# Seven PSUM banks of an attention and expert kernel: by the slot at which a reader is due, instead of in turn, with new slot tables

## The reference

```python
x = x + mlstm(layernorm(x), ctx, ctx)            # 4 heads of 64, gates, decays, a norm
x1 = layernorm(x)
n1 = ln(x1)                                      # one block of attention and experts
probs = softmax(mean(n1) @ rw + rb)              # over M = 2 attentions of 16 heads of 16
att = softmax(q k^T / 4) v, for each m and head; out = sum_m probs[m] * (att wo[m] + bo[m])
y = x1 + out
n2 = ln(y); p, i = top_k(softmax(mean(n2) @ ffn_rw + ffn_rb), 2)
x = x + y + sum_k p[k] * gelu(n2 @ fw1[i[k]]) @ fw2[i[k]]
```

## Time and profile before

| | |
|---|---|
| median of three runs | 1423.33 us (1421.33 to 1429.55) |
| profiled execution | span 1426.9 us, granted clock 0.990; the page has no other time of it |
| to the first score | 85.7 us |
| first period | 145.2 us |
| middle periods | 166.8, 167.1, 169.7, 167.1, 167.3, 167.2 us |
| last period's 128 scores | 133.1 us |
| after them | 57.7 us |
| busy share PE, DVE, ACT, POOL | 98%, 77%, 64%, 25% |

### The profile page before, as it was taken

How to read it: one execution, slowest core, us unless ns; L and a number is a source line. 1 busy time by engine, 2 the same in 40 slices (tenths; PEclk the granted TensorE clock), 3 DMA queues, 4 the chain that set the end, 5 groups by cost and what they waited for, 6 DMA issues and landing times.

```text
span 1426.9 us, 22218 instructions
## 1 busy us (share of the span) xinstructions
PE 1393.6 (98%) x7666; PEld 716.9 (50%) x7666; DVE 1092.2 (77%) x2299; ACT 916.4 (64%) x1706; POOL 363.6 (25%) x351
## 2 busy tenths in 40 slices
PE   8999899999999999999999999999999999999999
PEld 5643434455454654555445554455545454454456
DVE  5779977987789877987779877797769986786721
ACT  3266557766677666675677765876666766757752
POOL 6512342203313123132241133130331322330000
PEclk9999999999999999999999999999999999999999
DMA  4056037430854127441464308541084413561002
GB/s 116 17 70 95 2 45 107 71 62 16 104 76 76 45 38 112 75 75 31 51 101 69 64 31 101 79 75 46 24 102 70 78 56 45 73 77 46 17 1 89
DMA packets 92308, 90.15 MB, mean 63 GB/s; under 512 B 16483, under 2 KB 87267, under 8 KB 91295
## 3 DMA queue, kind: packets, MB, share of 16 engines
q1 hardware_dynamic: 92196, 88.73, 38.6%
HBM read 35.05 MB, written 4.25 MB: 28 GB/s over the span
## 4 chain that ended last, share of the span: by engine, by line
PE 69%; issue 8%; DVE 4%; DMA 3%; SPq 2%; POOL 1%; ACT 1%; DVEq 0%; POOLq 0%; ACTq 0%
PE psum L881 12%; PE psum L866 12%; PE psum L851 12%; PE psum L819 7%; PE psum L838 6%; PE psum L701 5%; PE psum L452 5%; PE psum L736 3%; DMA qst<-mrow 3%; PE psum L475 2%; SPq L1954 2%; PE psum L563 2%; DVE mx L1378 1%; PE psum L573 1%; DVE x L1293 1%
## 5 line engine op out<-in xcount | busy, mean ns | idle before, releaser
L1378 DVE TENSOR_REDUCE mx<-psum 128x1 f32<-128x512 f32 x1024 | 645.5, 681 | 134.2 <-PE psum L851 133.5
L1677 ACT ACTIVATE prob<-psum 128x512 f32<-128x512 f32 x1024 | 568.2, 600 | 270.8 <-PE psum L881 159.4
L866 PE MATMUL psum<-qst,kst 98*128 98x512 bf16 x1024 | 355.9, 383 | 10.5 <-DMA qst<-mrow 8.7
L851 PE MATMUL psum<-kst,qst 96*128 96x512 bf16 x1024 | 318.8, 381 | 2.9 <-DVE resid L1252 1.3
L881 PE MATMUL psum<-prob,vst 128*17 128x512 f32 x2048 | 248.1, 601 | 2.7 <-ACT prob L1677 2.3
L866 PEld LDWEIGHTS psum<-qst,kst 98*128 98x128 bf16 x1024 | 96.9, 99 | 220.8 <-issue 126.9
L851 PEld LDWEIGHTS psum<-kst,qst 96*128 96x128 bf16 x1024 | 99.0, 98 | 121.2 <-issue 17.9
L881 PEld LDWEIGHTS psum<-prob,vst 128*17 128x17 f32 x2048 | 46.7, 97 | 136.3 <-issue 106.8
L838 PE MATMUL psum<-w,cxT 128*128 128x256 f32 x448 | 105.4, 381 | 0.0
L819 PE MATMUL psum<-n2T,x 128*128 128x512 f32 x224 | 103.0, 592 | 0.0
L1828 POOL CAST parts<-resid 128x512 bf16<-128x512 f32 x64 | 41.0, 640 | 239.9 <-DVE resid L1252 239.9
(11 more groups left out here) (244 smaller groups left out, 1761.5 us busy)
## 6 DMA issues: line engine op xcount, KB each, us to landing
kst<-parts SPq DMA_DIRECT2D x186, 128.0 KB, 4.7
qst<-parts SPq DMA_DIRECT2D x186, 128.0 KB, 5.9
cmat<-G_dram SPq DMA_DIRECT2D x7, 1024.0 KB, 4.6
x<-in_L_ffn_fw SPq DMA_DIRECT2D x14, 512.0 KB, 3.7
w<-in_L_ffn_fw SPq DMA_DIRECT2D x14, 512.0 KB, 4.2
xbuf<-in_x SPq DMA_DIRECT2D x8, 512.0 KB, 5.1
kin<-in_ctx SPq DMA_DIRECT2D x8, 512.0 KB, 4.5
out<-acc SPq DMA_DIRECT2D x7, 512.0 KB, 9.0
```

The source lines that it names most:

```text
L851: e.matmul(psum[:, u.bank, :], qst[0:KROWS, h, t * P:(t + 1) * P], kst[0:KROWS, h, :], start=True, stop=True).then_inc(u.full, 1)
L866: e.matmul(psum[:, u.bank, :], kst[0:KROWS + 2, h, g * P:(g + 1) * P], qst[0:KROWS + 2, h, :], start=True, stop=True).then_inc(u.full, 1)
L1378: e.tensor_reduce(mx[:, qq * QUAD + j, t:t + 1], psum[:, u.bank, :], AX, ALU.max).then_inc(u.free, 1)
L1677: e.activation(prob[:, g % 2, j, :], psum[:, u.bank, :], ACT.Exp).then_inc(u.free, 1)
```

## The change

Each use now gets the bank whose last use has the earliest due slot (until), the longest unused one among equals; TensorE waits for that bank's last use. The due slot of a side piece's use is the slot of its reader in the tables (freed_at), at least the slot after the take; that of any other use is the slot after the take, and before the first slot all are equal. The values' bank is bank 7 instead of 6. All tables are new, for PE, ACT, DVE, POOL and SP, and so is AHEAD. VectorE's max_index waits for the expert loads of the batch before. What is computed is the same. Cut to what the prediction speaks of (the tables of POOL, SP and the second half, and ACT's others, are new in the same way):

```diff
 class Use:
-    def __init__(self, bank, n, full, free):
-        self.bank, self.n, self.full, self.free = bank, n, full, free
-class Ring:
-    def __init__(self, banks, full, free):
-        self.banks, self.full, self.free, self.n, self.uses = banks, full, free, 0, {}
-    def take(self, *name):
-        k, n = self.n % len(self.banks), self.n // len(self.banks)
-        self.n += 1
+    def __init__(self, bank, n, full, free, was, until):
+        self.bank, self.n, self.full, self.free, self.was, self.until = bank, n, full, free, was, until
+class Banks:
+    def __init__(self, count, full, free):
+        self.count, self.full, self.free, self.uses = count, full, free, {}
+        self.counts, self.latest, self.order, self.taken = [0] * count, [None] * count, [-1] * count, 0
+    def until(self, k):
+        return self.latest[k].until if self.latest[k] is not None else -1000
+    def take(self, name, until):
         assert name not in self.uses
-        self.uses[name] = Use(self.banks[k], n + 1, self.full[k], self.free[k])
-        return self.uses[name]
+        k = min(range(self.count), key=lambda k: (self.until(k), self.order[k]))
+        self.counts[k] += 1
+        self.taken += 1
+        self.order[k] = self.taken
+        use = Use(k, self.counts[k], self.full[k], self.free[k], self.latest[k], until)
+        self.uses[name] = self.latest[k] = use
+        return use
...
-        RB, VB = (0, 1, 2, 3, 4, 5, 7), 6
-        bank_full = [sem(f"bank_full_{k}") for k in range(len(RB))]
-        bank_free = [sem(f"bank_free_{k}") for k in range(len(RB))]
-        ring = Ring(RB, bank_full, bank_free)
-        uses = ring.uses
+        VB = 7
+        bank_full = [sem(f"bank_full_{k}") for k in range(VB)]
+        bank_free = [sem(f"bank_free_{k}") for k in range(VB)]
+        banks = Banks(VB, bank_full, bank_free)
+        uses = banks.uses
...
         FIRST = dict(
-            PE_A=slots(-8, "kT0:4 kT1:0 qT0:0 qT1:0 gates:7 gsum:18 cols:26 cd0:0 cd1:3 st0:0 st1:0 st2:0 num0:4 num1:4 "
-                       "num2 num3:25 n1T0 n1T1:0 p0:2 p1:15 p2 p3:13 pv0:9 pv1:0 logits"),
+            PE_A=slots(-8, "kT0:4 kT1:0 qT0:0 qT1:0 gates:7 gsum:19 cols:25 cd0:0 cd1:3 st0:0 st1:0 st2 num0 num1:5 "
+                           "num2 num3:26 n1T0:0 n1T1 p0 p1:7 p2:9 p3:14 pv0:11 pv1:0 logits"),
...
-            DVE_A=slots(-8, "bn0:0 bn1:0 bn2:0 bn3:0 var:0 qn0:0 qn1:0 qn2:0 qn3:13 fa:4 lf F:5 g:2 G:0 M:4 cols:2 "
-                        "gend:5 dec:17 decexp:0 cds0:3 cds1:0 cds2:0 cds3:0 sts0:0 sts1:2 sts2:0 num0:4 num1:0 "
-                        "sum1:0 m10:0 hc0:9 num2:0 sum2:0 num3:0 sum3:0 m11:0 hc1:0 norm:0 v0 v1:8 bn20 bn21:0 bn22 "
-                        "bn23:0 var2:7 n1q0:0 n1q1:0 n1q2:0 n1q3:5 s0:2 s1:14 s2:3 s3:4 mean:14 logits:2 mexp"),
+            DVE_A=slots(-8, "bn0:0 bn1:0 bn2:0 bn3:0 var:0 qn0:0 qn1:0 qn2:0 qn3:13 fa:3 lf F:6 g G:2 M:4 cols gend:14 "
+                            "dec:9 decexp:0 cds0:0 cds1:4 cds2:0 cds3:0 sts0:3 sts1:0 sts2:0 num0:0 num1 sum1:3 m10:0 "
+                            "hc0 num2:3 sum2:0 num3:0 sum3:0 m11:0 hc1:2 norm:2 v0:0 v1:8 bn20:0 bn21:0 bn22:2 bn23:0 "
+                            "var2:5 n1q0 n1q1:0 n1q2 n1q3:3 s0:4 s1:13 s2:2 s3:15 mean:7 logits:0 mexp"),
...
-            ACT_A=slots(-8, "kT0:4 kT1:0 qT0:3 qT1:0 gpart:4 grow1 grow0:2 fa:17 mask00:2 mask01:0 mask02:0 mask03:0 "
-                        "mask10:0 mask11 mask12:12 mask13:0 mask20 mask21:0 mask22:2 mask23:0 mask30:0 mask31:2 "
-                        "mask32:3 mask33:0 decexp:13 sq0:2 sq1:23 n1T0:0 n1T1 p0:2 p1:15 p2:0 p3:14 pv0:9 pv1:0 "
-                        "logits"),
+            ACT_A=slots(-8, "kT0:4 kT1:0 qT0:3 qT1:0 gpart:5 grow1:0 grow0:2 fa:20 mask00:0 mask01:0 mask02:0 mask03:0 "
+                            "mask10:0 mask11:0 mask12:0 mask13:5 mask20:4 mask21 mask22:0 mask23:2 mask30 mask31:0 "
+                            "mask32:5 mask33:2 decexp:12 sq0:4 sq1:22 n1T0:0 n1T1 p0 p1:7 p2:8 p3:15 pv0:10 pv1 logits"),
...
-            AHEAD="4143012020000224123001040240032140102140001323000001210101000000"
-                  "0011230310000010100132201121102102130131100104100010110002000000")
+            AHEAD="3243112020011105203000250133101500123010040211000003000310000030"
+                  "0010040500000100100214302020021500000100000200300013212002000000")
...
         MIDDLE = dict(
-            PE_A=slots(3, "kT0:5 kT1:2 qT0:0 qT1 gates:2 gsum:17 cols:14 cd0:2 cd1:7 st0:0 st1:0 st2 num0:4 num1:4 "
-                       "num2:0 num3:23 n1T0:0 n1T1:3 p0:5 p1 p2:6 p3 pv0:24 pv1:0 logits"),
+            PE_A=slots(5, "kT0:4 kT1 qT0:0 qT1 gates:2 gsum:16 cols:17 cd0:0 cd1:5 st0:0 st1:0 st2:2 num0:8 num1:0 "
+                          "num2:2 num3:23 n1T0:0 n1T1 p0:5 p1 p2:7 p3:2 pv0:25 pv1:0 logits"),
...
-            PE_C=slots(3, "cxT00:5 cxT01:2 cxT10:0 cxT11:4 wo0:0 wo1 wo2:4 wo3:16 mean:11 n2T0 n2T1:4 logits:8 hid00:0 "
-                       "hid01 hid02 hid03 eo00:6 eo01:0 eo02:2 eo03:5 hid10 hid11 hid12:0 hid13:4 eo10:3 eo11:2 "
-                       "eo12:8 eo13"),
+            PE_C=slots(-1, "cxT00:0 cxT01:13 cxT10:0 cxT11:2 wo0 wo1:0 wo2:5 wo3:17 mean:5 n2T0:3 n2T1:7 logits:6 hid00 "
+                           "hid01:0 hid02:2 hid03:2 eo00:2 eo01:2 eo02:0 eo03:7 hid10 hid11:0 hid12:0 hid13 eo10:3 "
+                           "eo11:5 eo12:11 eo13"),
...
-            DVE_A=slots(3, "bn0:0 bn1:0 bn2:0 bn3:0 var:3 qn0:0 qn1:3 qn2:0 qn3:4 fa lf F:2 g:3 G M:8 cols:0 gend:8 "
-                        "dec:8 decexp:0 cds0:0 cds1 cds2 cds3:3 sts0:0 sts1 sts2:3 num0:4 num1:0 sum1:0 m10 hc0:3 "
-                        "num2 sum2:0 num3:0 sum3:0 m11 hc1:0 norm v0 v1:11 bn20:0 bn21:0 bn22:0 bn23 var2:3 n1q0:0 "
-                        "n1q1:0 n1q2:0 n1q3:8 s0:4 s1:3 s2:5 s3:22 mean:4 logits:0 mexp"),
+            DVE_A=slots(2, "bn0:0 bn1:0 bn2 bn3:0 var qn0:0 qn1:0 qn2:3 qn3:6 fa lf:0 F g:4 G:2 M:8 cols:0 gend:10 "
+                           "dec:5 decexp:0 cds0 cds1:3 cds2:0 cds3:3 sts0:0 sts1 sts2 num0:7 num1:0 sum1:0 m10 hc0:0 "
+                           "num2:0 sum2:2 num3:0 sum3:0 m11 hc1:0 norm:0 v0 v1:12 bn20:0 bn21 bn22:0 bn23:0 var2:3 "
+                           "n1q0:0 n1q1:0 n1q2:2 n1q3:5 s0:4 s1:2 s2:6 s3:27 mean:0 logits:0 mexp"),
...
-            DVE_C=slots(14, "wo0:0 wo1 wo2:4 wo3:5 bn0 bn1:0 bn2:3 bn3:5 var:6 n20:0 n21:4 n22:0 n23:5 mean:2 logits:3 "
-                        "topk:9 acc00:5 acc01 acc02 acc03:12 acc10:3 acc11 acc12:9 acc13"),
+            DVE_C=slots(14, "wo0:0 wo1 wo2:6 wo3:4 bn0:0 bn1:3 bn2:0 bn3:3 var:5 n20:0 n21 n22:3 n23:7 mean:6 logits:0 "
+                            "topk:10 acc00:3 acc01:0 acc02:0 acc03:11 acc10:3 acc11:5 acc12:11 acc13"),
...
-            AHEAD="4111100000341233103011200000010312202101012000110120000020414420"
-                  "0001030121230210102104021021103012203101111110111012100002000000")
+            AHEAD="1300200300314230044012000010100221221000031300001011000104403001"
+                  "0020100321400001210130341010440001130110030202100012010003000000")
...
         LAST = dict(
-            PE_C=slots(5, "cxT00:3 cxT01:2 cxT10 cxT11:2 wo0 wo1 wo2:3 wo3:22 mean:7 n2T0:0 n2T1:3 logits:9 hid00 "
-                       "hid01:0 hid02:0 hid03 eo00:8 eo01 eo02:6 eo03:2 hid10:51 hid11:2 hid12:0 hid13:0 eo10:2 "
-                       "eo11:0 eo12:0 eo13"),
+            PE_C=slots(-1, "cxT00:9 cxT01 cxT10:3 cxT11:2 wo0:0 wo1 wo2:4 wo3:28 mean:0 n2T0:0 n2T1:3 logits:9 hid00 "
+                           "hid01:0 hid02:0 hid03 eo00:6 eo01:2 eo02:7 eo03:3 hid10:48 hid11:4 hid12:0 hid13:2 eo10:0 "
+                           "eo11:0 eo12 eo13"),
...
+        def freed_at(now, kind, b, *which):
+            if now < 0:
+                return now
+            tag = "".join(map(str, which))
+            period, key, piece = {
+                "kT": (b - 1, "ACT_A", kind + tag), "qT": (b - 1, "ACT_A", kind + tag), "n1T": (b - 1, "ACT_A", kind + tag),
+                "gparts": (b - 1, "ACT_A", "gpart"), "gates": (b - 1, "ACT_A", "grow0"), "cols": (b - 1, "DVE_A", "cols"),
+                "cd": (b - 1, "DVE_A", "cds" + tag), "st": (b - 1, "DVE_A", "sts" + tag),
+                "num": (b - 1, "DVE_A", "num0" if tag == "0" else "sum" + tag), "cross": (b - 1, "DVE_A", "num" + tag[0:1]),
+                "mlogits": (b - 1, "DVE_A", "logits"),
+                "proj": (b, "DVE_S", "s" + tag) if which[0:1] > (3,) or (b, tag) == (0, "3") else (b - 1, "DVE_A", "s" + tag),
+                "v": (b, "ACT_S", "v" + tag[1:]) if tag[0:1] == "1" else (b, "ACT_S", "pv" + tag[1:]) if b == 0 else
+                (b - 1, "ACT_A", "pv" + tag[1:]),
+                "cxT": (b + 1, "ACT_C", kind + tag), "wo": (b + 1, "DVE_C", kind + tag), "n2T": (b + 1, "ACT_C", kind + tag),
+                "flogits": (b + 1, "DVE_C", "logits"), "hid": (b + 1, "ACT_C", kind + tag), "eo": (b + 1, "DVE_C", "acc" + tag),
```

(15 more changed lines are left out.)

73 lines of the change are left out of this document (37 added, 36 removed).

## The result

The changed kernel takes 1409.18 us at the median (1405.8 to 1416.04), the kernel before 1422.89 beside it: a ratio of 0.9907, 95% interval 0.988 to 0.9934. That is 13.7 us for the 10 that were forecast. The same statement has a line number about 30 higher in the changed kernel: L895 is the score (L866 before), L880 the maximum (L851), L910 the values (L881), L1411 VectorE's maximum (L1378), L730 a projection (L701), L848 hid (L819), L867 eo (L838), L1283 the rest of a projection, which VectorE reads from its bank (L1252). L819 is here the mean of n2 in the end, which needs L1357, VectorE's normalising.

What follows compares the result with a forecast made beforehand. TensorE's own rate was taken to set the time, so only bubbles can be won: -4.3 - 4.2 - 1.0 - 1.6 - 0.9 + 1.8 = -10.2 us, off the median of 1423.33 giving 1413; range 1400 to 1427.

Steps and rivals of the forecast that it cites:

- The bank rule, 0: All periods: choosing banks by due slot changes almost no take, priced at 0; bounds -8.4 and +4.2 us.
- the ring: The old bank order, banks taken in turn: each take gets the bank of seven takes ago; no size of its own.
- First period, slot 96, -4.3: First score's wait for its two maxima rows covered by p2 and more maxima, slow clock behind gone: -4.3 us, bounds 0 and -4.8.
- Middle slot 96, -0.7 each: Six middle periods: the 0.78 us row wait covered by p0's move and more maxima: -4.2 in all, bounds 0 and -4.7.
- cds0, +0.3 each: Six middle periods, slots 44 to 46: VectorE waits at cds0 for the later cd0: +1.8 us in all, bounds 0 and +3.6.
- bank waits 0: Middle periods: about 1.4 us of bank waits each stay as they are, since the count of tight takes hardly moves: 0.
- First period, slots 65 to 71, -1.0 and -1.6: Exponential's wait at slot 65 shortened, -1.0 us; maxima's wait at slots 69 to 71, -0.8, and half the slow clock behind, -0.8.
- The end, -0.9: Before the last values: hid11, moved from slot 129 to 127, fills TensorE's 0.91 us idle: -0.9, bounds 0 and -0.9.
- Rival 1: The waits only move to other readers; some -3 us is left, 1420 us; chance 0.27.
- Rival 3: Slower: VectorE stands at cds0 in every middle period and TensorE with it; 3.2 us a period gives 1431; chance 0.11.
- rival 2: All goes well: every gain near its bound, half the bank waits gone, no cost at cds0: -19.0, 1404 us; chance 0.12.
- The weighed rule of the Trainium skill: Whole kernel: cycling PSUM banks swings the clock, so better bank choice would return clock lacking in the 0.990 mean; not counted.

Runs made afterwards that it cites:

- p2 late: The changed kernel with the first period's projection p2 back in slot 102 (it was moved to 93), nothing else undone: 1411.96 us, ratio 0.993 to the kernel before.
- projection slack: The changed kernel with the due slot of a projection's bank taken one slot later: 1407.65 us, ratio 0.9898 to the kernel before.

## Why the prediction was right, and where it was not

The time and its sign were right, the sum behind it only in part. The middle periods gave three times their term, within the first period two errors cancel, and in the last one a gain and a loss that were not foreseen stand against each other. That 10 came as near to 13.7 is partly luck.

- **The bank rule, 0.** Right for what was priced, the rule with the old slots: +0.6 (-1.1 to +2.4). Wrong as a term of this change. That 328 of 338 takes get the ring's bank with the new slots was read as nearly the ring, and the ten takes that differ hold 4.0 us of each middle period. The rule and the slots are one change: the rule without the slots is worth nothing, the slots without the rule can't run, by their order, or cost 20 us, both win 13.7. A count of takes has no price in it; one take of a bank whose reader is late cost 2.53, and the clock behind it some 1.5.
- **First period, slot 96, -4.3.** Right in size: slots 90 to 103 lose 1.6 us in the changed kernel and 5.2 to 6.6 in four kernels with the old first slots. p2 is the larger part, as said: undone alone, 2.8 by the medians and 4.0 in these slots. But what was left was taken for 0.5 us of row wait, and it is 1.22 for ScalarE. The prediction moved p2 on TensorE and did not follow it to ScalarE, where its copy (93 in that table too) needs a buffer that the loads of piece 0 still read. The wait changed its engine, not its cause.
- **Middle slot 96, -0.7 each.** Right: at slot 96 the row wait is gone in all six (0.19 us lost in one), and its 0.78 with it. But 1.3 us of it stand in the last slot of the sixth middle period, the whole row of the waits above; the kernel with the middle slots alone loses 1.5 there too. Behind it the clock is 0.50 for 3.4 us in both. It comes and goes: five kernels with the same middle and last slots have no such wait.
- **cds0, +0.3 each.** Wrong, it is 0. VectorE's arrival was taken from the earlier trace rows as if its order ahead of cds0 stayed; now an exponential of the decays holds it 0.70 us and its copy comes behind, so cd0 is done when it arrives.
- **The middle periods beside slot 96: bank waits 0, and nothing for cd.** Mis-sized; this is where the extra gain lies. A middle period is 1.4 us shorter with the middle slots (994.8 for 1003.3 over six), of which the row wait is some 0.8. With the old slots and the new rule the losses over 0.15 us outside slot 96 and the pieces themselves are 0.23 in slot 1, 0.18 in 35, 0.22 in 42, 0.18 in 61; none of them is there with the new ones. New are 0.26 in slot 57, 0.27 in 67 and, in most periods, up to 1.0 in slot 7 (0.4 on average with the middle slots alone), so that banks won and banks lost nearly cancel. What is left is mostly cd, which the sum had as a cost alone. Its 32 matmuls held TensorE for 2.86 us in every middle period with the old slots, in two blocks, and hold it for 1.99 as one (445.21 to 447.20 above): 0.87 less, of which the wait for a bank inside was 0.26. All this was read off traces, and no run took these slots one by one.
- **First period, slots 65 to 71, -1.0 and -1.6.** The wait for an exponential fell from 1.42 to 0.2, so that term holds. The second fails: TensorE waits 1.19 and 0.68 us for maxima in slots 69 and 70, no less than the earlier trace rows, and the clock behind is 0.64 for 3.5 us (165.5 to 169.0). That clock differs from execution to execution: with the same two waits "p2 late" and "projection slack" have 1.00 there, and slot 71 loses 0.24 us for 1.54. Together slots 60 to 75 lose 4.6 to 5.9 with the old first slots and 3.2 to 5.7 with the new ones, some 0.8 less for 2.6.
- **Not in the sum:** slots 14 to 39 of the first period, where TensorE lost 3.8 us in each of four kernels with old first slots and loses 1.6. I had read only the longest waits of that period, and this stretch has many of 0.2 to 0.8. It makes good what slots 69 to 71 lack: the first period is 7.3 and 8.6 us shorter with the new first slots in the traces (144.7 to 137.4, 145.4 to 136.8), and -6.4 by the medians, for -6.9.
- **The end, -0.9.** Wrong: 0.91 won and 1.72 paid, +0.4 for the whole stretch less the clock's share, and no difference between the medians with and without the new last slots. The step that hid11 fills the gap is right, and incomplete: eo10 in the same line went the other way, past the wait that it covered. Not in the sum: the last period's scores, 1.5 us shorter, as the rows of the last slots alone show.

Rival 1 was right of the end, where a wait moved, and of 1.22 us at slot 96 of the first period. Rival 3 did not appear. Of rival 2 some bank waits went, and about as many came.

The weighed rule of the Trainium skill ("TensorE: Matmul & The Clock Gate", section "A second HAM failure mode: psum-queue depth-cycling") would have the cycling of banks itself cost clock. The runs disagree for this kernel: with the old slots a middle period has 1.00 as before, with the new ones 1.00, and the clock fell behind single waits, of 1.26 us in the head, 2.46 at slot 96, 2.53 in slot 9 and, by the 0.97 there, 2.58 in the end.

The prediction's own reading, that the clock falls behind single long waits only, is too narrow. In the kernel before the stretch behind the last score has 0.97 too, and the longest wait there is 0.91 us. With the rule alone two waits of 0.69 us, at slots 60 and 61 of the first period, have 0.53 behind them for 3.5 us.

## What to carry to other kernels

A choice of buffers and a table of slots are one design: price them together, by following the few takes whose buffer changes, and ask for each how late its reader really is, not where the plan has it. When a piece is moved, follow it on every engine that handles it, and ask which wait it used to cover where it stood. Before one execution's end or head is compared with another's, take the clock's share off both. An instruction far off the critical path can lengthen one that is on it: look for a longest duration far above the median of its line.
